# Taking the repeated matmuls out of TensorE's waits, in a kernel that weaves attention, FFN and RWKV

## The reference

```python
x = L0_attn_x
x = x + _layernorm(_L0_attn_ref(_layernorm(x, axis=-1), ...), axis=-1)
x = x + _layernorm(_L0_ffn_ref(_layernorm(x, axis=-1), ...), axis=-1)
x = x + _layernorm(_L1_attn_ref(_layernorm(x, axis=-1), ...), axis=-1)
x = x + _layernorm(_L1_ffn_ref(_layernorm(x, axis=-1), ...), axis=-1)
```

```python
gate = jax.nn.sigmoid(local @ gl_w + remote_h @ gr_w)
mixed = gate * local + (1.0 - gate) * remote_h
return mixed.transpose(0, 2, 1, 3).reshape(B, S, D) @ out_w + out_b
```

```python
bonus = jnp.exp(u + k_t)[..., :, None] * v_t[..., None, :]
o_t = jnp.einsum('bhi,bhij->bhj', r_t, s + bonus)
s = jnp.exp(w_t)[..., None] * s + k_t[..., :, None] * v_t[..., None, :]
...
o = (o - mu) * jax.lax.rsqrt(var + EPS) * ln_w + ln_b
return (o * r).reshape(b, t, d) @ W_o.T
```

## Time and profile before

| | |
|---|---|
| median of 3 runs | 2293.34 us (2285.94 to 2295.15) |
| the profiled execution | 2294.64 us, its span 2292.8 us |
| busy in the span | TensorE 1842.8 us (80%), VectorE 1607.1 (70%), ScalarE 852.3 (37%), GpSimd 701.2 (31%) |
| busy time of the repeats (L1061) | 109.6 + 103.0 us |
| mean granted TensorE clock | 0.886 |
| a loop pass | about 201 us: the end of the FFN's residual (L598) stands at 245.8 us in batch 0 and at 1655.8 us in batch 7 |

### The profile page before, as it was taken

One profiled execution on the slowest core, in us unless ns is written; L12 is line 12 of the kernel. 1 busy time (PEld: TensorE's weight loads), 2 busy tenths in 40 slices (PEclk: granted clock), 3 DMA queues, 4 the chain that ended last, 5 costly groups with the idle time before them and its releaser, 6 DMA issues. The chain is left out here.

```text
span 2292.8 us, 32504 instructions
## 1 busy us (share of the span) xinstructions
PE 1842.8 (80%) x10626; PEld 1163.0 (51%) x10626; DVE 1607.1 (70%) x3353; ACT 852.3 (37%) x1804; POOL 701.2 (31%) x619
## 2 busy tenths in 40 slices
PE   0887998899799889979987997898666652499978
PEld 0454454455445445544544554454434442499963
DVE  3224589669758866976896697689669965477745
ACT  0242443345334333524442353334322222366632
POOL 0000033114103311420330141033018873466641
PEclk9777989899999998989999998989886666699989
DMA  4000000000000000000000000000103234576666
GB/s 136 0 1 10 0 1 1 20 1 1 10 11 1 1 20 1 1 10 11 1 1 20 1 1 10 11 1 1 32 15 109 100 111 141 198 247 187 182 215 267
DMA packets 83763, 119.77 MB, mean 52 GB/s; under 512 B 12729, under 2 KB 70397, under 8 KB 83456
## 3 DMA queue, kind: packets, MB, share of 16 engines
q1 hardware_dynamic: 69376, 80.59, 11.5%
q0 software_dynamic: 13056, 35.68, 4.2%
q10 hardware_dynamic: 1152, 1.18, 0.1%
HBM read 67.71 MB, written 51.79 MB: 52 GB/s over the span
## 5 line engine op out<-in xcount | busy, mean ns | idle before, releaser
L653 DVE TENSOR_TENSOR_SCAN s_buf<-r_work,kvb 128x512 f32<-128x512 f32 x256 | 352.8, 1380 | 0.0
L838 POOL TENSOR_TENSOR p_buf<-s_buf,r_work 128x512 f32<-128x512 f32 x128 | 152.9, 1195 | 458.4 <-DVE s_buf L653 451.0
L911 ACT ACTIVATE probs<-bank_s,nmx 128x256 f32<-128x256 f32 (+1 forms) x512 | 186.6, 450 | 110.3 <-DVE nmx L516 109.3
L838 POOL TENSOR_TENSOR r_work<-s_buf,r_work 128x512 f32<-128x512 f32 x128 | 158.4, 1239 | 191.7 <-DVE s_buf L653 191.4
L803 POOL TENSOR_TENSOR rstd<-vare,mhalf 128x4 f32<-128x4 f32 x48 | 48.4, 1008 | 509.9 <-DVE vare L449 509.9
L929 ACT ACTIVATE pt<-bank_s 128x1024 f32<-128x1024 f32 (+1 forms) x128 | 117.4, 918 | 216.7 <-PE bank_s L1219 216.7
L642 DVE TENSOR_TENSOR kvb<-r_work,bank 128x512 f32<-128x512 f32 x256 | 174.5, 682 | 21.6 <-PE bank L1337 13.3
L516 DVE TENSOR_REDUCE nmx<-bank_s 128x4 f32<-128x1024 f32 (+1 forms) x128 | 137.5, 1074 | 48.0 <-PE bank_s L1169 47.7
L1896 POOL DMA_INDIRECT y_rows<-w_in_ys,m_y_idx x144 | 141.7, 984 | 89.7 <-ACT w_in_ys L1982 53.8
L1061 PE MATMUL bank_s<-wmask,ident_b 128*128 128x512 bf16 x356 | 109.6, 465 | 44.4 <-DVE vare L449 28.5
L1336 PE MATMUL bank<-v_hi,sel_v 128*128 128x512 f32 x256 | 132.1, 516 | 14.8 <-DVE kvb L642 8.1
(11 more groups left out here) (403 smaller groups left out, 4204.8 us busy)
## 6 DMA issues: line engine op xcount, KB each, us to landing
m_xs<-x_rows SPq DMA_DIRECT2D x146, 144.0 KB
w_lo<-y_rows SPq DMA_DIRECT2D x4, 2048.0 KB, 21.9
w_hi<-y_rows SPq DMA_DIRECT2D x4, 2048.0 KB, 23.3
w_in_ys<-in_w SPq DMA_DIRECT2D x17, 256.0 KB, 3.9
x_new<-in_x SPq DMA_DIRECT2D x8, 512.0 KB, 3.7
x_after_rwkv<-x_b SPq DMA_DIRECT2D x8, 512.0 KB, 3.8
m_x_all<-x_after_rwkv SPq DMA_DIRECT2D x8, 512.0 KB, 4.1
out<-m_x_all SPq DMA_DIRECT2D x8, 512.0 KB, 3.0
```

The lines of the kernel that those rows point to most:

```text
L653: V.tensor_tensor_scan(s_buf[:, n % 2, 1:S + 1], dec[:, n // HD, :], kvb[:, n % 2, :], 0.0, ALU.mult, ALU.add).then_inc(sem["state"], 1)
L838: G.tensor_tensor(p_slot(n), s_buf[:, n % 2, 0:S], rf[:, n // HD, :], ALU.mult).then_inc(sem["rs"], 1)
L911: ins = A(probs[:, n % 2, x, h * w:h * w + w], score_banks[n % 2][:, x, h * w:h * w + w], ACT.Exp, bias=nmx[:, n, 2 * x + h:2 * x + h + 1])
```

## The change

All calls of `repeat` go, with the waits that stood only for them. The function goes too. No other instruction, order or buffer changes.

```diff
@@ -1055,11 +1055,6 @@
             ins.then_inc(tern_tot, 1)
             pe.wait_ge(const_ready, 1)
 
-            def repeat(dst, n):
-
-                for _ in range(n):
-                    T.matmul(dst[:], ident_b[:], wmask[:].rearrange("p a m -> p (a m)"), start=True, stop=True)
-
             def turn(b, name, n, out_name, dst, src):
 
                 for k in range(NK):
@@ -1084,17 +1079,6 @@
 
             def attention_ffn(b):
                 yield "norm1"
-                if not (isinstance(b, int) and b == 0):
-                    pe.wait_ge(sem["var"], at(b, "var", 0))
-                    repeat(A3, 4)
-                    pe.wait_ge(sem["rstd"], at(b, "rstd", 0))
-                    repeat(A3, 8)
-                    pe.wait_ge(sem["a_final"], at(b, "a_final", 0))
-                    repeat(A3, 8)
-                pe.wait_ge(sem["var"], at(b, "var", 1))
-                repeat(A3, 4)
-                pe.wait_ge(sem["rstd"], at(b, "rstd", 1))
-                repeat(A3, 1)
                 turn(b, "normed", 0, "turned", (A0, A1), xn)
                 yield "turn1"
                 pe.wait_ge(sem["evened"], at(b, "evened", 2))
@@ -1222,12 +1206,6 @@
                         local_values(n - 1)
                     yield f"local{n}"
                 yield "gate"
-                pe.wait_ge(sem["loc"], at(b, "loc", QUADS))
-                repeat(A2, 6)
-                pe.wait_ge(sem["gate_z"], at(b, "gate_z", 1))
-                repeat(A2, 4)
-                pe.wait_ge(sem["gate_e"], at(b, "gate_e", 1))
-                repeat(A2, 8)
                 pe.wait_ge(sem["mixed"], at(b, "mixed", 1))
                 for k, dst in enumerate((A0, A1)):
                     for i in range(NT):
@@ -1240,16 +1218,6 @@
                 yield "out"
                 yield "resid1"
                 yield "norm2"
-                pe.wait_ge(sem["var"], at(b, "var", 2))
-                repeat(A4, 4)
-                pe.wait_ge(sem["rstd"], at(b, "rstd", 2))
-                repeat(A4, 8)
-                pe.wait_ge(sem["x_free"], at(b, "x_free", 1))
-                repeat(A4, 8)
-                pe.wait_ge(sem["var"], at(b, "var", 3))
-                repeat(A4, 4)
-                pe.wait_ge(sem["rstd"], at(b, "rstd", 3))
-                repeat(A4, 1)
                 turn(b, "normed", 1, "turned", (A0, A1), xn)
                 yield "turn2"
 
@@ -1270,7 +1238,6 @@
                                            stop=f == NF - 1 and c == 1)
                     ins.then_inc(sem["f_y"], 1)
 
-                repeat(A4, 5)
                 pe.wait_ge(sem["f_lo"], at(b, "f_lo", 1))
                 for f in range(NF + 2):
                     if f < NF:
@@ -1322,7 +1288,6 @@
                 proj(3)
                 yield "rproj3"
                 pe.wait_ge(sem["dec"], at(b, "dec", 2))
-                repeat(R1, 6)
                 pe.wait_ge(sem["rb"], at(b, "rb", 1))
                 for g, dst in enumerate((R1, R2)):
                     ins = T.matmul(dst[:], headones[:], r_work[:, 10 + g, :], start=True, stop=True)
@@ -1369,7 +1334,6 @@
                     yield f"wait{i}"
                 yield "o_norm"
                 pe.wait_ge(sem["o_var"], at(b, "o_var", 1))
-                repeat(R1, 8)
                 pe.wait_ge(sem["o_norm"], at(b, "o_norm", 1))
                 for g, dst in enumerate((R2, R0)):
                     for i in range(NT):
```

## The result

The median after is 2330.68 us (2318.21 to 2333.46, four runs), against 2294.09 us of the kernel before beside it (2285.94 to 2295.15, four runs): a ratio of 1.0154, 95% interval 1.0131 to 1.0177. The forecast was 2344, the range 2312 to 2374, slower at 0.85; the kernel became slower by 36.6 us where some 50 were expected.

What follows compares the result with a forecast made beforehand. TensorE was taken to bound FFN and projections, VectorE the scan; 6.4 us a pass times seven (44.8), batch 0 +7.8, last RWKV batch -1.5 made +51.1 us, about 2344 us against the median, range 2312 to 2374.

Steps and rivals of the forecast that it cites:

- three ramps a pass: Low clock after dense work begins at gate, FFN and projections; each ramp loses 1.55 to 3.0 us, taken as 2.3.
- Output norm: RWKV output norm: 8 repeats delay the transposes in a stretch without gaps; removal gives back 1.74 us per pass.
- First norm: First norm and projections, with the 4 behind the FFN: slower transposes 0.55 plus ramp 2.3, 2.9 us a pass.
- Gate: Before mixing: slower transposes 0.88 plus ramp 2.3, less VectorE's slack of 1.77, gives 1.4 us a pass.
- Second norm and FFN: Slower turn 0.55 plus FFN ramp 2.3, less the 1.74 coming back in that stretch: 1.1 us a pass.
- Bonus and scan: Without the bonus's 6 repeats the clock falls every second pass, costing the scan stage 1.0 us a pass (0 to 4.3).
- price of 0.43 us per microsecond of low clock: Scan stage: cost per microsecond at half speed, from lengths of 97.4 and 101.7 us at mean clocks 0.98 and 0.93.
- Batch 0: Batch ahead of the loop: no slack at the gate, ramps at FFN and projections; +7.8 us together (4.5 to 11).
- Last RWKV batch: After the loop: part of eight repeats' 3.61 us comes back, transposes and projection run slower; -1.5 us (-2.7 to 0).
- The low clock is covered: Rival, faster: ramps fall where TensorE is not awaited, only the 13.7 us direct gain stays, about 2280; chance 0.07.
- Transposes wake the clock: Rival, no change: transposes bring the clock up before dense work; -4.3 us over seven passes, about 2289; chance 0.08.
- slower still: Rival: clock falls at every bonus gap and small matmuls keep it low in the scan; +23 us, about 2367; chance 0.15.

Runs made afterwards that it cites:

- kernel of narrow repeats: Kernel before with all 708 repeats and all waits kept, each repeat writing 16 columns instead of 512; 2320.74 us, ratio 1.0111.
- kernel of four places: Kernel before without the output norm's 8 repeats and the 4 behind the FFN; 2272.15 us, ratio 0.9918.
- kernel of three places: Kernel before with repeats only at gate (18), second norm (25) and first norm (25); 2295.63 us, ratio 1.0004.
- Taking out the surplus as well: Kernel of four places with the first 12 of the 25 first-norm repeats also out; 2268.92 us, ratio 0.9892 against the kernel before.
- latent repeats: Kernel of three places plus two repeats after each of the first three token tiles of the latent product; 2304.38 us, ratio 1.0041 against the kernel before.

## Why the prediction was right

**The mechanism.** The time went where it was put: three ramps a pass, one direct gain. The kernel of narrow repeats shows that it is the clock and not the waits: with every wait and every repeat in place, only narrower, 27.2 us are lost of the kernel after's 36.6. Between the two profiled executions the scan stages (6.9 us) and batch 0 (7.3) differ most, the two parts that also move without an edit.

**Output norm, 1.74 us a pass.** Right, 1.74 measured alone.

**First norm, 2.9.** 2.7 in the kernel after, 2.8 alone.

**Gate, 1.4.** 1.3 alone, 0.9 in the kernel after. VectorE waits 0.93 us for the output matmuls in the pass shown, after 1.77 us of slack were used up. One reading behind it is too wide: the pattern of a low clock that the repeats raise stood before the mixing transposes in five of the seven passes before. In the other two, the one at 595 us in the earlier trace rows among them, the clock was at 1.00 all through the gate with the repeats in place.

**Second norm and FFN, 1.1.** 1.3 in the kernel after: 0.5 in the turn (7.3 to 7.8) and 2.5 in the ramp, (228.7 - 211.3) / 7, less 1.74. The ramp's middle value of 2.3 was right as a mean of unlike passes: the FFN of the first two lost 1.5 us (31.7 against 30.2), that of the last four 2.9. With the second norm's repeats alone taken out it lost 1.6 (234.6 - 223.5, by seven). Why the clock comes back after 3 us in one pass and after 6 in another is not settled.

**Bonus and scan, +1.0 a pass: the term that was mis-sized.** It measured -0.5. The step "a low clock for 4.55 us costs 2.0; every second time makes 1.0" took the scan stage's level from before as given and added to it. The level isn't given. Before, it swings between 97.4 and 101.7 with the length of the low clock in the latents (3.4 to 13.7 us); after, two passes fell at the bonus and took 101.0, and the last four settled at 98.5. Windows of the first scan stage and a later one of the kernel after:

```profile
299.90:400.90 101.00, 91.28 (x699) 53.51 (x707) 91.41 (x103) 44.65 (x92) 42.33 (x34) 0.93 0.00 1
...
922.20:1020.70 98.50, 87.49 (x699) 51.77 (x707) 91.02 (x104) 44.61 (x92) 43.07 (x34) 0.97 0.00 1
```

So the term is 10.5 of the 12.3 us by which the profile's sum missed, and that it came out on the cheap side is luck: nothing in the prediction foresaw on which lengths the passes would settle. Its price of 0.43 us per microsecond of low clock was of the right size (some 0.34, last section); what failed is the sum of low clock, which fell from 71.5 to 65.1 us over the seven stages, where the forecast added 16. The price of the bonus's repeats lies between nothing (taken out of the kernel before) and 1.8 us a pass (12.9 us by seven, out of the kernel of four places), by how the rest of the pass falls.

**Batch 0, +7.8.** 9.2 from its first statistics on, inside the bounds of 4.5 to 11, but only half of it can be laid to the change. 4.4 us lie from the gate on, where repeats had stood: 2.3 up to L565, 0.5 at the second norm's turn, 1.5 in the FFN. The other 4.8 lie ahead of the gate, where kernels that leave this part as it was differ among themselves by 6.4 us (128.8 to 135.2). With the gate's repeats alone out, the stretch up to L565 grew by 1.0 us, not by the 3.2 of the forecast. **Last RWKV batch, -1.5.** The rest after the loop gave -2.7, but three kernels that change nothing there take 630.4 to 637.9 us for it (before 635.8), so the runs can't show this term.

**The rivals.** "The low clock is covered" falls: the projections lost 19 us of 281.5. "Transposes wake the clock" falls: after the turns the clock was still 0.50, in both places of every window shown. (Its 0.55 + 0.55 - 1.74 makes -4.5 us over seven passes, not -4.3; nothing hangs on it.) The Trainium skill (TensorE: Matmul & The Clock Gate, Part 4: PE-mode transpose), which says that transposes don't bring the full clock, agrees with the clock of these windows. The losses of the loop outside the scan, 19.0 + 6.2 + 8.8 and the 12.2 that came back, are 46.2 us, 2.0% of 2292.8, slow transposes included. The Trainium skill's rule for modelling (TensorE: Matmul & The Clock Gate, Part 1, section What's actually happening), that the rise costs under 1% of a typical kernel's span, does not carry over to this kernel, which pays for three rises in each of seven passes. Of "slower still" the first half was seen: in two passes of seven of the kernel after the clock fell at the bonus, but it was back after 3.4 us, and these stages (101.0) are no longer than the longest before (101.7). Its premise was one-sided: in batch 0 the clock did come back, at 130.1 us, right behind the window of the earlier trace rows and amid the same small work.

**What the prediction lumped.** The change took out repeats of four kinds: those that raise the clock (most of those at the norms and, in most passes, at the gate), those that hold it over a short wait (the five ahead of the FFN, the six at the bonus), those that only stand in the way (the eight), and those that do nothing (in the loop, the four behind the FFN and twelve at the first norm). The prediction counted the five ahead of the FFN to the first kind; its sum did not suffer, as both go together here. The kernel of three places, built on that reading, gained nothing (1.0004), but its time does not price the five: with them back, and the bonus's six still out, it is 0.9985 (0.9967 to 1.0003), an interval that overlaps. What the five are worth shows in the FFN stretch, 15.8 us over seven passes.

## What to carry to other kernels

Price a dummy matmul by what the stretch behind it does: it is worth its ramp where dense work bound by TensorE follows a wait, it can hold the clock over a wait of 2 us, and it costs its full length where TensorE has no gap. Read each place on its own, and take out first those that only stand in the way: here that alone gave 0.992. Taking out the surplus as well gave 0.9892, which the intervals do not part from it. And don't take the level of a later stage as fixed when an earlier one changes its length.

## What the hardware showed that was not expected

**The fall comes after the wait.** In the kernel of three places the FFN's first two matmuls still run at the full clock and the slow ones come behind them, in the middle of dense work. The fall behind a wait of 2.06 us is thus charged later, to instructions that waited for nothing.

**The clock falls while TensorE is busy.** In the pass of 101.7 us of the kernel before, the clock is at 0.50 for 13.7 us in the latents although TensorE is busy in all of it. It falls amid 64x16 products, of which TensorE does 32 in a row (22 of them in the row below), and 128x512 products behind them take 0.63 to 0.79 us. The windows ahead of the fall and in it, and the timeline of TensorE there:

```profile
889.90:901.50 11.60, 9.45 (x57) 6.79 (x56) 9.82 (x13) 4.56 (x7) 2.21 (x2) 1.00 0.01 1
901.50:915.20 13.70, 13.70 (x48) 8.35 (x48) 9.24 (x11) 1.46 (x5) 4.88 (x5) 0.50 0.00 0
```

```profile
899.76 3.27 PE L1152 MATMUL bank<-rv_sb,work 64*128 64x16 f32 x22
902.95 0.79 PE L1336 MATMUL bank<-v_hi,sel_v 128*128 128x512 f32 x1
903.54 0.63 PE L1337 MATMUL bank<-v_lo,sel_v 128*128 128x512 f32 x1
```

**One stage, few lengths.** The length goes with the sum of low clock in the stage, wherever in it the clock is low; the latents' stretch is one part, and from some 95 us on, at the stage's end, stand another 0.8 to 3.4 us in most passes. In all runs the scan stage without latent repeats takes 96.6 us with no low clock at all, 97.3 to 97.6 with 3.4 us of it, 98.1 to 98.5 with 6.3 to 6.8, 99.7 to 99.8 with 9.8 to 10.2 (once 100.2), 100.2 to 100.4 with 11.1 to 11.5, 100.5 to 100.6 with 13.2 to 13.6 and 101.0 to 101.8 with 13.7 to 15.1. Over these 91 stages that is about 0.34 us per microsecond of low clock, an estimate by a straight line through them. VectorE is busy for some 91 us of each. Passes can settle on a length and keep it: the last four of the kernel after take 204.7 to 204.8 us each. Where the low stretch in the latents begins goes with its length: from 11.0 to 11.9 us behind L629 it lasts 6.8 or 13.7 us, from 12.3 to 13.6 mostly 3.4, from 13.8 to 15.0 again 10.2. So a shift of one or two us ahead of the stage moves its length: over the kernels that left the stage untouched, its sum runs from 685.5 to 699.4 us. What fixes the point of the fall stays open.
